# One attention stage of a two-layer kernel rewritten: 32 heads in one stream, key tiles in pairs, the next batch prepared in pieces inside heads

## The chip, the cores and the metric

The kernel runs on one core of one Trainium2 chip. The metric is the device time of one execution, in microseconds. PE is TensorE, PEld its weight load, DVE VectorE, ACT ScalarE, POOL GpSimd, SP SyncE, whose queue issues most DMAs.

## The reference, cut to what matters

Four steps add to x (4 batches of 512 rows, 256 columns): a cross-attention, a mixture of experts, a second cross-attention, a second mixture. The change is in the second cross-attention:

```python
# x: (4, 512, 256), ctx: (4, 1601, 256); 8 heads of 32; Wq, Wk, Wv: (256, 256)
query = _layernorm(x, axis=-1)
q = _split_heads(query @ Wq.T, 8)
k = _split_heads(ctx @ Wk.T, 8)
v = _split_heads(ctx @ Wv.T, 8)
attn = jax.nn.softmax(jnp.einsum('bhnd,bhmd->bhnm', q, k) * 32 ** (-0.5), axis=-1)
x = x + jnp.einsum('bhnm,bhmd->bhnd', attn, v).transpose(0, 2, 1, 3).reshape(B, Nq, C)
```

## The kernel before, in words

`build` calls `attention0`, `experts`, `attention1` and `experts` one after the other; each has its own blocks of engine programs with semaphores written by hand. The stage in question is `attention1`. Numbers are held as sums of two float16 parts, high and low, so that a float32 product becomes three float16 matmuls (`triple`).

Per batch it needs: the context turned (`cth`, `ctl`; 13 tiles of up to 128 rows, the last has 65), keys (`khs`, `kls`), values (`vst`), and, for each head, stacked operands: `kst` holds high, low and high part of the keys on 96 partitions, `qst` high, high and low part of the queries, so that one matmul over 96 rows gives the whole score. Row 97 of `qst` holds the negative row maximum and row 97 of `kst` ones, so the score matmul subtracts the maximum as well. The stacking is done by DMAs from SP, `kst` 24 per batch (L1735), `qst` 24 once for all four batches (L1727).

Order of the work before: an opening normalises all 16 tiles of x (L2040 to L2048), turns weights and x (L1872, L1877), makes all queries (L1859 to L1861) and prepares batch 0. In the function `event(b, i)` the steps of a batch are numbered: 8 turn the context, 8 make keys, 13 make values. Turn and key steps of the next batch run inside the last head of a batch (`NEXT`). The value steps and the stacking of keys run between batches, since there is one `vst` and one `kst`. Then `pre` computes the maxima of the batch's first head (12 matmuls of 512 columns L1962, four of 65 L1955, into two PSUM banks `psA`; DVE reduces them, L2108, L2103, L2093; PE turns the result, L1946; DVE writes it to `qst`, L2097), and the heads run in a loop.

A head (`main`) goes over 13 key tiles. For each, PE makes a score (L1995) into one of four banks `psS`; ACT takes the exponential twice, into float32 `pf` (L1831) and float16 `ph` (L1833); POOL (10 tiles, L1774) or DVE (tiles 2, 6 and 10, L2130) subtracts them to the low part `pl`. Five tiles later PE multiplies the values with `ph` and `pl` into `psO` (L1971, L1973). Beside it runs `pre` for the next head. At tile 5 ACT copies the previous head's `psO` to `of` (L1820), PE folds it (L1983) and DVE divides and adds to X (L2113, L2117). The heads 1 to 6 of a batch are a hardware loop over registers; the batches too.

Of the kernel before, what the change touches and what calls it, by code (L numbers as in the profile page):

```python
# [1592 lines left out]
def attention1(nc, X, identf, io):  # L1593

# [11 lines left out]
    NCK = len(KCH)  # L1606
    NQ = KC * NT // 4 + G * B
    NGC = KC * -(-JT // 4)
    NV0 = NGC + G * NCK
    NW = NV0 + JT  # L1610
    NA = 1 + ST * (NCK - 1)
# [3 lines left out]
    LAG = 5  # L1615
    PR = ring(JT, 7)
    SR = ring(JT, 4)
    R, NS = max(PR) + 1, max(SR) + 1
    VT = [2, 6, 10]
    GT = [j for j in range(JT) if j not in VT]  # L1620

    with ExitStack() as ctx:
        def sb(name, shape, dt=F32):
            return ctx.enter_context(nc.sbuf_tensor("c_" + name, shape, dt))

        def sem(name):
# [16 lines left out]
        cth, ctl = sb("cth", [P, KC, M], F16), sb("ctl", [P, KC, M], F16)  # L1643
        mx, mc = sb("mx", [P, ST, NCK]), sb("mc", [P, ST])
        pf = sb("pf", [P, R, S])
        ph, pl = sb("ph", [P, R, S], F16), sb("pl", [P, R, S], F16)
        of = sb("of", [VC, S])
        fold = sb("fold", [VC, DH + 1])
        rl = sb("rl", [P, ST])

        psA = [ctx.enter_context(nc.psum_tensor(f"c_psA{i}", [P, 512], F32)) for i in range(2)]
        psS = [ctx.enter_context(nc.psum_tensor(f"c_psS{i}", [P, 512], F32)) for i in range(NS)]
        psO = ctx.enter_context(nc.psum_tensor("c_psO", [P, 512], F32))
        psM = ctx.enter_context(nc.psum_tensor("c_psM", [P, 512], F32))
        ring4 = psA + psS[0:2]
# [3 lines left out]
        s_cx = sem("cx")  # L1659
        s_st = sem("st")  # L1660
        s_mv = sem("mv")
        s_pool = sem("pool")
        s_rstd = sem("rstd")
        s_nt = sem("nt")
        s_uP = sem("uP")
        s_uH = sem("uH")
        s_uL = sem("uL")
        s_q = sem("q")
        s_wP = sem("wP")
        s_wH = sem("wH")  # L1670
# [38 lines left out]
        NONE = [[] for _ in range(JT)]
# [503 lines left out]
```

## Time and profile before

| | us |
|---|---|
| median of 3 runs | 2967.51 (2966.61 to 2968.86) |
| the profiled execution | 2967.55 |
| its span, first to last instruction | 2965.7 |
| mean granted TensorE clock | 0.932 |

| engine | busy us | share |
|---|---|---|
| PE | 2521.8 | 85% |
| PEld | 1505.1 | 51% |
| DVE | 1938.1 | 65% |
| ACT | 1728.1 | 58% |
| POOL | 1535.5 | 52% |

The profile is of one execution. Busy shares are means over four stages; names of tiles begin with `a_` in the first attention, `f_` in the experts and `c_` in the second attention. A releaser ("<-") is what ended an idle time. Matmuls overlap: the busy time of one is longer than its distance to the next.

### The profile page before, as it was taken

The numbers are of one execution on the slowest core, as the hardware profiler recorded it, in microseconds if no ns is written. First come the engines' busy times: TensorE is split into PE (matmuls) and PEld (weight loads), VectorE is DVE, ScalarE is ACT, GpSimd is POOL, SyncE is SP. The second block draws the span as 40 slices with busy tenths as digits, with TensorE's granted clock in tenths as the row PEclk, the third lists the DMA queues.
The fourth block names the chain that finished last, engine by engine and source line by source line (L and its number), as shares of the span: only waits on it lengthen the run. The fifth ranks groups of instructions, "written<-read, shape, count | busy, mean of one in ns | idle before, by whom it ended". The sixth has DMA issues, their size and how long they took to land. (4 is left out here: it accounts for less than half of the span.)

```text
span 2965.7 us, 51867 instructions
## 1 busy us (share of the span) xinstructions
PE 2521.8 (85%) x15253; PEld 1505.1 (51%) x15380; DVE 1938.1 (65%) x3676; ACT 1728.1 (58%) x3155; POOL 1535.5 (52%) x1359
## 2 busy tenths in 40 slices
PE   4999999999999999999945991688888888379992
PEld 2455555555555555555424881344344444258882
DVE  5778677776777776677754644675767677656443
ACT  3556656566555665555523750387786868357661
POOL 2576766676676765665744005075665747320004
PEclk9999999999999999999966995799898999579996
DMA  4000000000000000000025413401002010543113
GB/s 130 1 1 1 23 1 1 1 1 23 1 1 1 1 1 1 1 1 1 1 89 180 146 39 97 99 1 30 26 3 52 0 34 0 203 160 117 45 46 93
DMA packets 83500, 122.54 MB, mean 41 GB/s; under 512 B 11139, under 2 KB 67285, under 8 KB 83349
## 3 DMA queue, kind: packets, MB, share of 16 engines
q1 hardware_dynamic: 72020, 86.23, 9.7%
q0 software_dynamic: 9472, 30.16, 3.0%
q10 hardware_dynamic: 1856, 4.19, 0.4%
q8 instruction: 89, 1.46, 0.2%
q14 instruction: 63, 0.51, 0.1%
HBM read 73.23 MB, written 34.34 MB: 36 GB/s over the span
## 5 line engine op out<-in xcount | busy, mean ns | idle before, releaser
L396 POOL TENSOR_TENSOR a_acc<-a_acc,a_pf 128x512 f32<-128x512 f32 (+1 forms) x480 | 644.8, 1343 | 388.0 <-ACT a_pf L524 367.8
L1774 POOL TENSOR_TENSOR c_pl<-c_pf,c_ph 128x512 f16<-128x512 f32 x320 | 386.8, 1227 | 284.7 <-ACT c_ph L1833 282.3
L524 ACT ACTIVATE a_pf<-a_psS 128x1024 f32<-128x1024 f32 (+1 forms) x288 | 281.2, 976 | 303.6 <-PE a_psS L663 300.1
L813 DVE TENSOR_TENSOR a_pl<-a_pf,a_ph 128x512 f16<-128x512 f32 x448 | 404.6, 912 | 27.5 <-ACT a_ph L530 27.5
L789 DVE TENSOR_REDUCE a_mx<-a_psA 128x1 f32<-128x512 f32 x512 | 344.5, 684 | 49.0 <-PE a_psA L600 42.7
L1270 POOL DMA_INDIRECT f_xn<-f_yrows,f_gidx x64 | 60.7, 949 | 506.5 <-DMA f_yrows<-f_xn 487.6
L1831 ACT ACTIVATE c_pf<-c_psS 128x512 f32<-128x512 f32 (+1 forms) x416 | 255.9, 615 | 114.0 <-PE c_psS L1995 110.6
L2108 DVE TENSOR_REDUCE c_mx<-c_psA 128x1 f32<-128x512 f32 x384 | 251.3, 684 | 53.0 <-PE c_psA L1962 51.2
L530 ACT ACTIVATE a_ph<-a_psS 128x1024 f16<-128x1024 f32 (+1 forms) x288 | 281.0, 976 | 0.0
L1833 ACT ACTIVATE c_ph<-c_psS 128x512 f16<-128x512 f32 (+1 forms) x416 | 257.4, 619 | 0.0
L784 DVE TENSOR_TENSOR a_vl<-a_psA,a_vh 128x256 f16<-128x256 f32 (+1 forms) x272 | 115.0, 423 | 167.4 <-ACT a_vh L469 164.4
L1130 DVE TENSOR_TENSOR f_xn<-f_xn 128x256 f16<-128x256 f32 x320 | 132.3, 422 | 130.9 <-ACT f_xn L1106 126.4
L685 PE MATMUL a_psO<-a_pl,a_vh 128*128 128x512 f16 (+1 forms) x544 | 206.7, 380 | 6.9 <-POOL a_pl L401 6.9
L679 PE MATMUL a_psO<-a_ph,a_vh 128*128 128x512 f16 (+1 forms) x544 | 206.9, 380 | 1.0 <-DVE a_ol L818 1.0
L542 PE MATMUL a_psS<-a_qh,a_kh 128*128 128x512 f16 (+1 forms) x544 | 206.6, 380 | 0.9 <-ACT a_mrow L485 0.8
L680 PE MATMUL a_psO<-a_ph,a_vl 128*128 128x512 f16 (+1 forms) x544 | 206.7, 380 | 0.0
L543 PE MATMUL a_psS<-a_ql,a_kh 128*128 128x512 f16 (+1 forms) x544 | 206.7, 380 | 0.0
L544 PE MATMUL a_psS<-a_qh,a_kl 128*128 128x512 f16 (+1 forms) x544 | 206.5, 380 | 0.0
L600 PE MATMUL a_psA<-a_kh,a_qh 128*128 128x512 f16 x512 | 194.3, 380 | 4.7 <-DVE a_kl L778 1.2
L778 DVE SCALAR_TENSOR_TENSOR a_kl<-a_psA,a_bkv,a_kh 128x512 f16<-128x512 f32 (+1 forms) x160 | 105.3, 658 | 133.7 <-ACT a_kh L463 133.6
L1035 PE MATMUL f_psH<-f_xh,f_w 128*128 128x256 f16 x648 | 178.4, 275 | 15.3 <-ACT f_xn L1106 11.7
L1971 PE MATMUL c_psO<-c_ph,c_vst 128*65 128x512 f16 (+1 forms) x416 | 160.8, 386 | 22.7 <-ACT c_of L1820 22.7
(340 smaller groups left out, 6395.2 us busy)
## 6 DMA issues: line engine op xcount, KB each, us to landing
f_stage<-in_L_ffn_w SPq DMA_DIRECT2D x16, 1024.0 KB
f_stage<-in_L_ffn_W SPq DMA_DIRECT2D x16, 1024.0 KB
f_xn<-f_xrows SPq DMA_DIRECT2D x41, 256.0 KB, 2.8
f_yrows<-f_xn SPq DMA_DIRECT2D x40, 256.0 KB, 2.2
c_kst<-c_khs SPq DMA_DIRECT2D x64, 100.1 KB, 2.2
f_xrows<-f_zero POOLq DMA_DIRECT2D x1, 6400.0 KB, 26.4
a_cx<-in_ctx SPq DMA_DIRECT2D x4, 1536.0 KB
c_cx<-in_ctx SPq DMA_DIRECT2D x4, 1536.0 KB
```

Of the source, the lines that this page charges most:

```text
L396: g.tensor_tensor(acc[0:k, p, :], acc[0:k, p, :], pf[0:k, q % RF, i, :], ALU.add).then_inc(s_acc, 1)
L524: act.activation(pf[0:r, q % RF, 0:k, :], psS[q % 2][0:r, 0:k, :], ACT.Exp, scale=SCALE).then_inc(s_pF, 1)
L530: act.activation(ph[0:r, q % RP, 0:k, :], psS[q % 2][0:r, 0:k, :], ACT.Exp, scale=SCALE).then_inc(s_pH, 1)
L543: pe.matmul(out, hi, xl_, start=False, stop=False)
L679: pe.matmul(psO[:, :], vh[0:r, g % 2, j, vs], ph[0:r, q % RP, i, :], start=(j == 0), stop=False)
L680: pe.matmul(psO[:, :], vl[0:r, g % 2, j, vs], ph[0:r, q % RP, i, :], start=False, stop=False)
L789: v.tensor_reduce(mx[:, n % 2, it, c:c + 1], ps[:, 0:KCH[c][1]], AX.X, ALU.max).then_inc(s_fr, 1)
L813: v.tensor_tensor(pl[0:r, q % RP, i, :], pf[0:r, q % RF, i, :], ph[0:r, q % RP, i, :], ALU.subtract).then_inc(s_pL, 1)
L1774: g.tensor_tensor(pl[0:r, PR[j], :], pf[0:r, PR[j], :], ph[0:r, PR[j], :], ALU.subtract).then_inc(s_pG, 1)
L1831: act.activation(pf[0:r, PR[j], :], psS[SR[j]][0:r, :], ACT.Exp, scale=SCALE).then_inc(s_pF, 1)
L1833: act.activation(ph[0:r, PR[j], :], psS[SR[j]][0:r, :], ACT.Exp, scale=SCALE).then_inc(s_pH, 1)
L2108: v.tensor_reduce(mx[:, it, c:c + 1], psA[what % 2][:, 0:cn], AX.X, ALU.max).then_inc(s_aF, 1)
```

## The change

`attention1` is written anew; the other stages are the same to the letter.

- The 32 heads form one stream with no loop: every instruction is written out. The unit is a pair of key tiles (6 pairs and the last tile alone, `UNITS`). `psS` becomes two buffers of two banks, and each exponential covers a pair. `psA` has three banks, used in turn by all steps (`ALL`, `IDX`); `psM` is gone.
- `kst`, `qst` and `vst` have two buffers. `qst` is made per batch, so 48 stacking DMAs per batch go out, six for each head with a semaphore for each head (`s_stack`).
- The next batch is prepared in 25 steps at 22 places of heads 0 to 5 (`PREP_AT`): T turns a chunk of the context, K makes keys, V the values of a pair of tiles, N turns the normalised x, Q makes queries. The context comes in chunks of 512 rows through two buffers, one DMA each.
- The maxima of the next head (M, then L for the last 65 columns, X for the turning) stand at fixed places (`M_AT`). Values lag four units (eight tiles) instead of five tiles; `ph` and `pl` have seven pair buffers, `pf` four.
- The first `item` in the diff is PE's; `out_copy` is DVE's. Subtractions: DVE has two per head (`ON_DVE`), POOL eleven. The copy of `psO` goes from ACT to DVE (`out_copy`). DVE writes the divided output to `yt`, and POOL adds it to X (`add_to_x`).

```diff
-    LAG = 5
-    PR = ring(JT, 7)
-    SR = ring(JT, 4)
-    VT = [2, 6, 10]
+    UNITS = [(j, j + 1) for j in range(0, JT - 1, 2)] + [(JT - 1,)]
+    NB = 3
+    LAG, LATE, RF, RP = 4, 1, 4, 7
+    ON_DVE = {(4, 1), (5, 1)}
+    TOP = U - 1
+    def keys_and_values(b):
+        out = []
+        for c in range(NK):
+            out += [("T", b, c, k) for k in range(KC) if k < parts(c)]
+            out += [("K", b, c, g) for g in range(G) if g < parts(c)]
+            out += [("V", b, u) for u in range(2 * c, min(2 * c + 2, U))]
+        return out
+    def queries(b):
+        return [("N", b, 0), ("N", b, 1), ("Q", b, 0), ("Q", b, 1)]
+    M_AT = [(0, 0), (0, 2), (0, 3), (1, 0), (1, 2), (2, 0), (2, 2), (2, 3), (3, 0), (3, 2), (4, 0), (4, 2)]
+    PREP_AT = [(h, u, p) for h in range(6) for u, p in ((1, 1), (4, 1), (5, 1), (6, 1))]
+    PREP_AT = [(h, u, p) for h, u, p in PREP_AT if (h, u) >= (0, LAG + 1)]
...
+            at[TOP - 1][0].append(("L", n + 1))
+            at[TOP - 1][3].append(("X", n + 1))
+        if n >= 1:
+            at[LAG][2].append(("F", n - 1))
...
-        kst = sb("kst", [P, H, M], F16)
+        kst = sb("kst", [P, 2, H, M], F16)
-        vst = sb("vst", [P, JT, H, VC], F16)
+        vst = sb("vst", [P, 2, JT, H, VC], F16)
-        cx = sb("cx", [P, JT, D])
+        cx = sb("cx", [P, 2, 4, D])
-        psS = [ctx.enter_context(nc.psum_tensor(f"c_psS{i}", [P, 512], F32)) for i in range(NS)]
-        psM = ctx.enter_context(nc.psum_tensor("c_psM", [P, 512], F32))
+        psA = [pb(f"psA{i}", [P, 512]) for i in range(NB)]
+        psS = [pb(f"psS{i}", [P, 2, S]) for i in range(2)]
...
+            for b in range(B):
+                for c in range(NK):
+                    load_context(b, c)
+                stack(b)
...
+            def add_to_x(n):
+                b, h = divmod(n, H)
+                g.wait_ge(s_fr, after_dve(("F", n)))
+                xs = X[:, b * ST:(b + 1) * ST, h * DH:(h + 1) * DH]
+                g.tensor_tensor(xs, xs, yt[:, n % 2, :, :], ALU.add).then_inc(s_x, 1)
...
+            def item(what):
+                i = IDX[what]
+                ps = psA[i % NB]
+                if i >= NB:
+                    pe.wait_ge(s_fr, i - NB + 1)
...
+                for u in range(U):
+                    q = uid(n, u)
+                    places = AT[n][u]
+                    values = tiles_of(q - LAG) if q >= LAG else ()
+                    for i in range(2):
+                        if i < len(UNITS[u]):
+                            score(n, u, i)
+                        for what in places[i]:
+                            item(what)
+                    for i in range(2):
+                        if i < len(values):
+                            value(q - LAG, i)
+                        for what in places[2 + i]:
+                            item(what)
...
+            def out_copy(n):
+                v.wait_ge(s_pv, uid(n, U - 1) + 1)
+                if n >= 1:
+                    v.wait_ge(s_it, IDX[("F", n - 1)] + 1)
+                v.tensor_copy(of[:, :], psO[0:VC, :]).then_inc(s_oF, 1)
```

How the instructions stand now at three places. First PE between two batches, before: the maxima of the batch's first head (L1955, L1962), their turning (L1946), and then the first scores (L1995), each with what it waits for in brackets.

```order
L1955 MATMUL c_psA<-c_kst,c_qst 128x65 [waits c_q,c_aF,c_k0,c_wL]
L1955 MATMUL c_psA<-c_kst,c_qst 128x65 x3
L1962 MATMUL c_psA<-c_kst,c_qst 128x512 [waits c_aF] x12
L1946 MATMUL c_psM<-identf,c_mc 1x128 [waits c_tF,c_mc]
L1946 MATMUL c_psM<-identf,c_mc 1x128 x3
L1995 MATMUL c_psS<-c_qst,c_kst 128x512 [waits c_mr,c_pH,c_k1]
L1955 MATMUL c_psA<-c_kst,c_qst 128x65 [waits c_aF]
L1955 MATMUL c_psA<-c_kst,c_qst 128x65 x3
L1962 MATMUL c_psA<-c_kst,c_qst 128x512 [waits c_aF]
L1995 MATMUL c_psS<-c_qst,c_kst 128x512 [waits c_pH]
L1962 MATMUL c_psA<-c_kst,c_qst 128x512 [waits c_aF]
```

Now the same place, the end of head 7 and the start of head 8: the turning (L1999), the last score of head 7 (L2017), values (L2034, L2039), the first score of head 8, and a maximum of head 9 (L1987).

```order
L1999 MATMUL c_psA<-identf,c_mc 1x128 [waits c_mc,c_fr]
L1999 MATMUL c_psA<-identf,c_mc 1x128 x3
L2017 MATMUL c_psS<-c_qst,c_kst 65x512 [waits c_pH]
L2034 MATMUL c_psO<-c_ph,c_vst 65x512 [waits c_pH]
L2039 MATMUL c_psO<-c_pl,c_vst 65x512 [waits c_pG,c_pL]
L2034 MATMUL c_psO<-c_ph,c_vst 65x512
L2039 MATMUL c_psO<-c_pl,c_vst 65x512
L2017 MATMUL c_psS<-c_qst,c_kst 128x512 [waits c_fr,c_pH]
L1987 MATMUL c_psA<-c_kst,c_qst 128x512 [waits c_stack1,c_fr]
L2017 MATMUL c_psS<-c_qst,c_kst 128x512
```

The block of twelve maxima in a row is gone; between the scores of two batches stand four value matmuls, and the wait is for the stacking of head 9, not of the whole batch.

Second, PE where the previous head's `psO` must have been copied (`c_oF`). Before, at tile 5 of a head: a value of the previous head (L1973), a score, a maximum, the new head's first value (L1971).

```order
L1973 MATMUL c_psO<-c_pl,c_vst 65x512 [waits c_pG]
L1992 REGISTER_ALU
L1995 ISA [waits c_pH]
L1995 MATMUL c_psS<-c_qst,c_kst 128x512
L1951 REGISTER_ALU
L1962 MATMUL c_psA<-c_kst,c_qst 128x512 [waits c_aF]
L1971 ISA [waits c_oF,c_pH]
L1971 MATMUL c_psO<-c_ph,c_vst 65x512
L1698 ISA
L1973 MATMUL c_psO<-c_pl,c_vst 65x512 [waits c_pG]
```

Now, in unit 4 of head 7 (one of a batch's two heads without preparation): a score, a maximum, a score, the first value (L2034), a maximum, the fold (L2004), the unit's second tile, and the next unit.

```order
L2017 MATMUL c_psS<-c_qst,c_kst 128x512 [waits c_pH]
L1987 MATMUL c_psA<-c_kst,c_qst 128x512 [waits c_fr]
L2017 MATMUL c_psS<-c_qst,c_kst 128x512
L2034 MATMUL c_psO<-c_ph,c_vst 65x512 [waits c_oF,c_pH]
L2039 MATMUL c_psO<-c_pl,c_vst 65x512 [waits c_pG,c_pL]
L1987 MATMUL c_psA<-c_kst,c_qst 128x512 [waits c_fr]
L2004 MATMUL c_psA<-c_fold,c_of 128x33 [waits c_oF,c_fr]
L2004 MATMUL c_psA<-c_fold,c_of 128x33 x3
L2034 MATMUL c_psO<-c_ph,c_vst 65x512
L2039 MATMUL c_psO<-c_pl,c_vst 65x512
L2017 MATMUL c_psS<-c_qst,c_kst 128x512 [waits c_pH]
L1993 MATMUL c_psA<-c_kst,c_qst 128x65 [waits c_fr]
```

In heads 1 to 5 a preparation step stands ahead of that first value, behind the second score. The copy itself has moved from ACT to DVE.

Third, SP. Before, the keys of a batch are the last of 24 DMAs; the load of the next batch's context follows.

```order
L1735 DMA c_kst<-c_khs 32x1601
L1741 REGISTER_ALU
L1717 ISA [waits c_wP]
L1717 DMA c_cx<-in_ctx 128x12x256
L1719 ISA
L1719 DMA c_cx<-in_ctx 65x256
L1738 REGISTER_ALU
```

Now the last of the 48 stacking DMAs of batch 0 (keys L1790 and queries L1791 in turn) and the first chunks of batch 1's context (L1776).

```order
L1790 DMA c_kst<-c_khs 32x1601 [waits c_fr]
L1791 DMA c_qst<-c_qhs 32x512
L1790 DMA c_kst<-c_kls 32x1601
L1791 DMA c_qst<-c_qhs 32x512
L1790 DMA c_kst<-c_khs 32x1601
L1791 DMA c_qst<-c_qls 32x512
L1776 DMA c_cx<-in_ctx 128x4x256 [waits c_it] x3
L1778 DMA c_cx<-in_ctx 65x256 [waits c_it]
```

So the first load for batch 1 has 48 issues ahead of it in SP's queue instead of 24 for keys alone (after 24 for queries).

## Rows read from the trace of the kernel before

**Rows 1.** Windows: busy us (x) of PE, PEld, DVE, ACT, POOL; clock, DMA share, GB/s.

```profile
1836.40:1882.70 46.30, 19.35 (x92) 12.37 (x92) 35.08 (x67) 11.02 (x19) 15.49 (x9) 0.67 0.17 53
1882.70:1926.00 43.30, 32.31 (x173) 17.73 (x173) 23.28 (x45) 14.16 (x30) 0.00 (x0) 0.79 0.69 168
1962.50:1978.30 15.80, 13.60 (x68) 6.85 (x67) 12.08 (x24) 13.61 (x28) 12.18 (x11) 1.00 0.00 0
2044.50:2064.00 19.50, 17.05 (x91) 8.24 (x90) 7.89 (x18) 13.15 (x28) 7.82 (x7) 1.00 0.07 16
2064.00:2087.00 23.00, 17.26 (x107) 10.47 (x107) 15.28 (x33) 6.95 (x15) 0.00 (x0) 0.82 0.63 166
2087.00:2107.30 20.30, 20.19 (x76) 7.77 (x76) 16.38 (x26) 18.03 (x37) 14.82 (x13) 0.78 0.00 0
```

**Rows 2.** Timeline at the first seam: start, length, instruction, [idle before <-what ended it].

```profile
2075.19 0.60 SPq L1735 DMA_DIRECT2D c_kst<-c_kls  x1
2075.83 0.60 SPq L1735 DMA_DIRECT2D c_kst<-c_khs  x1
2087.64 0.60 ACT L1831 ACTIVATE c_pf<-c_psS 128x512 f32<-128x512 f32 x1 [13.01 <-PE c_psS L1995]
```

**Rows 3.** Waits in three plain heads (1962.5 to 2010): total us, times, longest.

```profile
PE c_psM L1946 <- DVE c_mc L2093: 3.5, 3, 1.2
PE c_psO L1971 <- ACT c_of L1820: 2.5, 3, 0.8
```

**Rows 4.** Timeline, PE in a plain head.

```profile
1983.70 0.38 PE L1971 MATMUL c_psO<-c_ph,c_vst 128*65 128x512 f16 x1
1983.92 0.38 PE L1973 MATMUL c_psO<-c_pl,c_vst 128*65 128x512 f16 x1
...
1986.35 0.60 PE L1946 MATMUL c_psM<-identf,c_mc 128*1 128x128 f32 x4 [1.18 <-DVE c_mc L2093]
```

**Rows 5.** Timeline, ACT: 512 columns here, 1024 columns in the first attention.

```profile
368.71 1.02 ACT L524 ACTIVATE a_pf<-a_psS 128x1024 f32<-128x1024 f32 x1 [0.17 <-PE a_psS L663]
369.63 0.38 ACT L469 ACTIVATE a_vh<-a_psA 128x256 f16<-128x256 f32 x1
...
1985.38 0.67 ACT L1833 ACTIVATE c_ph<-c_psS 128x512 f16<-128x512 f32 x1
1985.86 0.68 ACT L1831 ACTIVATE c_pf<-c_psS 128x512 f32<-128x512 f32 x1
```

**Rows 6.** By source line: ns min/median/max of one, first and last start, forms.

```profile
L1774 POOL TENSOR_TENSOR c_pl<-c_pf,c_ph x320: 1147/1155/1609, 1928.0 to 2530.3; 128x512 f16<-128x512 f32 x160
L2130 DVE TENSOR_TENSOR c_pl<-c_pf,c_ph x96: 679/735/1643, 1931.1 to 2528.2; 128x512 f16<-128x512 f32 x96
L362 POOL TENSOR_TENSOR X<-X,a_yt x128: 716/728/1277, 155.4 to 1508.6; 128x256 f32<-128x256 f32 x128
```

**Rows 7.** Timeline: the opening of the second attention, and its last instruction.

```profile
1847.23 16.11 DVE L2048 TENSOR_SCALAR c_qst<-X,c_mv,c_rstd 128x256 f32<-128x256 f32 x16 [3.58 <-POOL c_rstd L1752]
...
1914.77 0.57 PE L1955 MATMUL c_psA<-c_kst,c_qst 96*128 96x65 f16 x4 [1.33 <-DVE c_vst L2082]
1925.97 0.59 PE L1995 MATMUL c_psS<-c_qst,c_kst 97*128 x1 [1.09 <-DVE c_qst L2097]
...
2533.94 0.73 DVE L2117 SCALAR_TENSOR_TENSOR X<-c_psM,c_rl,X 128x32 f32<-128x32 f32 x4
```

**Rows 8.** The page, DMA issues: KB each, median us from issue to landing.

```profile
c_kst<-c_khs SPq DMA_DIRECT2D x64, 100.1 KB, 2.2
a_vl<-in_L_xattn_Wq ACTq DMA_DIRECT2D x1, 1024.0 KB, 5.5
```

**Rows 9.** Timeline, PE at the lower clock level, after the seam.

```profile
2088.41 0.63 PE L1962 MATMUL c_psA<-c_kst,c_qst 96*128 96x512 f16 x1
2088.83 0.63 PE L1995 MATMUL c_psS<-c_qst,c_kst 97*128 x1
```

**Rows 10.** The page: TensorE's granted clock in tenths, 40 slices of 74.1 us.

```profile
PEclk9999999999999999999966995799898999579996
```

More of the change, by code:

```diff
@@ new lines, in last_turn, with last_keys, after_act, after_dve @@
+    def last_turn(b, c):
+        return IDX[("T", b, c, parts(c) - 1)]
+    def last_keys(b, g):
+        return max(IDX[("K", b, NK - 2, g)], IDX[("K", b, NK - 1, 0)])
+    def after_act(what):
+        return AH[IDX[what]]
+    def after_dve(what):
+        return IDX[what] + 1
+    PER_DVE = len(ON_DVE)
+    PER_POOL = JT - PER_DVE
+    def low_dve(q):
+        n, u = divmod(q, U)
+        return n * PER_DVE + sum(1 for w in range(u + 1) for i in range(len(UNITS[w])) if (w, i) in ON_DVE)
+    def low_pool(q):
+        n, u = divmod(q, U)
+        return n * PER_POOL + sum(1 for w in range(u + 1) for i in range(len(UNITS[w])) if (w, i) not in ON_DVE)
@@ L1647, in attention1 @@
         of = sb("of", [VC, S])
         fold = sb("fold", [VC, DH + 1])
[L1649 to L1655 removed]
+        rl = sb("rl", [P, 2, ST])
@@ new lines, in item, with score @@
+                ins.then_inc(s_it, 1)
+            def score(n, u, i):
+                q, j = uid(n, u), UNITS[u][i]
+                b, h = divmod(n, H)
+                r = rows1(j)
+                if i == 0:
+                    if q >= 2:
+                        pe.wait_ge(s_pH, q - 1)
+                    if u == 0:
+                        pe.wait_ge(s_fr, after_dve(("X", n)))
+                ins = pe.matmul(psS[q % 2][0:r, i, :], kst[0:KR, b % 2, h, j * P:j * P + r], qst[0:KR, b % 2, h, :],
+                                start=True, stop=True)
+                if i == len(UNITS[u]) - 1:
+                    ins.then_inc(s_sP, 1)
@@ new lines, in value @@
+            def value(q, i):
+                n, u = divmod(q, U)
+                b, h = divmod(n, H)
+                j = UNITS[u][i]
+                r = rows1(j)
+                if i == 0:
+                    pe.wait_ge(s_pH, q + 1)
+                    if u == 0 and n >= 1:
+                        pe.wait_ge(s_oF, n)
+                if h == 0 and i == 0:
+                    pe.wait_ge(s_fr, after_dve(("V", b, u)))
+                w = vst[0:r, b % 2, j, h, :]
+                pe.matmul(psO[0:VC, :], w, ph[0:r, q % RP, i, :], start=(j == 0), stop=False)
+                if i == 0:
+                    if low_dve(q):
+                        pe.wait_ge(s_pL, low_dve(q))
+                    pe.wait_ge(s_pG, low_pool(q))
+                ins = pe.matmul(psO[0:VC, :], w, pl[0:r, q % RP, i, :], start=False, stop=(j == JT - 1))
+                if i == len(UNITS[u]) - 1:
+                    ins.then_inc(s_pv, 1)
@@ new lines, in _ @@
+            norm(0, "xs")
+            norm(0, "xa")
+            norm(0, "nx")
+            for what in OPEN + FIRST:
+                item(what)
+            for n in range(NH):
+                b, h = divmod(n, H)
+                for u in range(U):
+                    q = uid(n, u)
+                    places = AT[n][u]
+                    if n >= 1 and u == LAG:
+                        out_copy(n - 1)
+                    for i in range(2):
+                        low(q - LATE, i)
+                        for what in places[i]:
+                            item(what)
+                    for what in places[2] + places[3]:
+                        item(what)
+                    if b + 1 < B and (h, u) in NORM_AT:
+                        norm(b + 1, NORM_AT[h, u])
@@ L2156, in build @@
+            for q in range(NH * U - LATE, NH * U):
+                for i in range(len(tiles_of(q))):
+                    low(q, i)
+            out_copy(NH - 1)
+            for what in CLOSE:
+                item(what)
 def build(nc, io, out, phases):
```

777 lines of the change are left out of this document (346 added, 431 removed).

## Prediction

> **What bounds the kernel now.** The change touches one stage of four, so I first cut the run by stage with the windows [rows 1]. The second attention lasts from 1836.4 us to the end of its last addition at 2534.7 [rows 7]: 698.3 of 2965.7. Its first score stands at 1926.0 [rows 7], so the opening takes 89.6 and the 32 heads 608.7. A plain head takes 15.8: PE is busy 13.6, ACT 13.6, POOL 12.2, DVE 12.1, at full granted clock. No engine is full. The reader should see the seam instead: 23.0 us (2064 to 2087) in which POOL does nothing and ACT 7.0, followed by a head at clock 0.78 that takes 20.3 instead of 15.8. ACT waits 13.0 for the first score of the new batch [rows 2]. Head 7, which prepares part of the next batch, takes 19.5 [rows 1]. Seven plain heads and such a seam make the batch 161 us, 34 more than eight plain heads.
>
> Then the waits of three plain heads [rows 3]: PE stands 1.2 us per head for the column maxima (`mc`) before the transposes, and 0.8 per head for the copy of psO. A matmul's busy time overlaps the next one's; what it costs PE is the start-to-start time, 0.217 us for 512 columns [rows 4].
>
> **Part by part.** *PE's work per head* is unchanged: 13 scores, 26 value and 12 maxima matmuls, 51 x 0.217 = 11.1; four transposes of mc 0.43 (four take 0.60, the last 0.27 of it is drain [rows 4]); four 65-column maxima 0.5 and four folds 0.9, both estimates from the same timeline. Sum 12.9, against 15.8 taken.
>
> *ACT.* 26 exponentials become 12 of 1024 columns and two of 512. Start to start, 1024 columns take 0.92, 512 take 0.48 [rows 5]: 12.0 us per head, where 26 x 0.48 = 12.5 plus a psO copy of 0.48 stood before. The copy goes to DVE, for which no row has a price; between ACT's 0.59 and a DVE subtraction of 0.74 [rows 6] I take 0.65, on DVE's 12.1 us [rows 1], which loses one subtraction and the four additions to X. DVE stays near 11.5.
>
> *POOL* gets 11 subtractions instead of 10, and the addition to X. Alone a subtraction takes 1.15, beside a DVE subtraction up to 1.61, and DVE's own then goes to 1.64 [rows 6]. I take 11 x 1.12 (start to start) + 2 x 0.4 for the two met by DVE's + 0.45 for an addition half as wide as the 0.73 one [rows 6]: 13.5 per head. Now a rule against this move: the Trainium skill's GPSIMD Engine Reference, section Key points, says that for elementwise work DVE is structurally about twice as fast. The trace agrees at 1.155 against 0.735. By the rule, with that one subtraction left on DVE, POOL's head would be 12.4. Either way POOL lies under the PE figure below, so the sum stands; the rule feeds the rival in which POOL leads.
>
> *Waits in a plain head.* Maxima come in pairs of units with three banks instead of two, and the last of them (65 columns) is followed by a score and four value matmuls before the transposes, 1.1 us, as long as DVE's two short reductions: the wait of 1.2 goes. The copy of psO stays: PE finishes the previous head's last value, issues one maximum, two scores and another (0.87) and then needs the copy, while DVE first reduces the maximum and then copies, some 1.9 from the same point. PE waits 1.0 to 1.1. With 0.2 for the rest a plain head takes 12.9 + 1.3 = 14.2. Bounds: POOL's 13.5, and today's 15.8.
>
> *Preparation in heads.* Per batch PE gets 36 matmuls of 512 (7.8) and twelve of 65 (0.4) for K, 78 of 256 columns at half the pitch (8.5) for V, 34 transposes at 0.108 (3.7), 12 of 512 (2.6) for Q: 23.0 us, in heads 0 to 5. Nothing hides these on PE, because PE is already the longest engine; they hide ACT's and DVE's share (25 steps of about 0.48 and 0.65). They also hide the psO copy in heads 1 to 5, where such a step stands ahead of the value. Heads 0 to 5 together: 6 x 12.9 + 23.0 + 1.1 + 6 x 0.25 = 103. In ACT's order a preparation copy stands between the two exponentials of a unit and waits for its own matmuls; I follow a unit: PE 3.0, ACT 0.92 + 0.7 idle + 0.48 + 0.92 = 3.0. It just fits, so the bounds are 16.9 and 19 per head.
>
> *The stream.* A batch is 103 + 2 x 14.2 = 131.4, three times 394; the last batch 7 x 14.2 + 12.0 (no maxima, ACT's time) = 111.4. The three seams disappear, because the next head's maxima find their stacked rows ready: SP starts the 48 stacking DMAs at the end of head 5, one each 0.64 us [rows 2], landing 2.2 later [rows 8]; head 0's six are in after 6 us, heads 6 and 7 last 28.
>
> One new wait, once. In batch 0 SP issues all 48 stacking DMAs (30.7 us) before the load of batch 1's first chunk, 512 KB, which lands some 4 later (1 MB took 5.5 [rows 8]). PE wants that chunk in unit 5 of head 0. With everything stacked from 1882.5 on, the chunk is there at 1917.5 and PE asks at 1909.5: 8 us. Behind the wait the clock falls, as it did after each seam; I add 4. In later batches the same 30.7 us end about 8 us ahead of the request. Draining the last units, fold and addition add 3. Together 394 + 111.4 + 8 + 4 + 3 = 520.4.
>
> *The opening.* Norms, transposes and Q of batch 0 alone: the scaling of 16 tiles, 16.1 us [rows 7], becomes 4, done by 1845 instead of 1863. Then 25 steps on PE, in three banks: 25 us of matmuls (the 23.0 above and the turning of the weights) plus five chains of 1.8 (a K or Q needs the DVE half of the transposes before it) plus 3 at the low clock, to 1882.5. Six DMAs and their landing 6.0; the first head's maxima took 11.2 (1914.8 to 1926.0 [rows 7]). First score at 1899.7, the opening 63.3 instead of 89.6. The two memsets of kst on POOL hide behind this; they end near 1862.
>
> Sum: 63.3 + 520.4 = 583.7 against 698.3, so 114.6 less. The profiled execution took 2967.55 (span 2965.7), the median of the runs is 2967.51, no different. 2967.5 - 114.6 = 2852.9; the first maxima at the low clock may cost a little more, so I say **2854**.
>
> **The rivals.**
> *Engines in step (chance 0.21).* In-order ACT and a POOL near 13.5 of 14.2 lose to each other what the seams give: plain heads stay at 15.8, preparing heads take 19. Stream 3 x (114 + 31.6) + 7 x 15.8 + 12 + 15 = 574.4, so 2967.5 - 60.6 = 2907. For it: before, PE also had 12.9 of work and took 15.8. Against it: there it waited for maxima, which now have room [rows 3].
>
> *Everything hides (0.12).* Plain heads at POOL's 13.5, preparing ones 16.9, no late chunk, an opening of 56: 3 x 128.4 + 106.5 + 3 = 494.7, so 2820.
>
> *The clock oscillates (0.04), slower than before.* At the lower level a matmul of 512 columns starts every 0.43 us [rows 9]; 51 of them take 21.9, a plain head about 24, 10 more. From twelve of the 32 heads on, the gain of 114 is gone; with all of them at 1.2 GHz, and 23 more in each of three batches, the run takes 2854 + 320 + 69 = 3243. For it: small waits in each head. Against it: the first attention, written in this same pattern, keeps the full level from slice 2 to slice 20 [rows 10]. The rule is in the Trainium skill, TensorE: Matmul & The Clock Gate, section A second HAM failure mode: psum-queue depth-cycling: a kernel that cycles through PSUM banks idles so often that its clock oscillates. The trace so far disagrees: plain heads cycle banks at 1.00 [rows 1].
>
> *The seam moves rather than goes (0.05).* If SP's 48 DMAs arrive late in every batch and not once, PE loses 8 + 4 twice more: 2878.
>
> **How the numbers follow.** The forecast has the remaining 0.58. Faster than by 0.2% (about 6 us, what a measurement of this kernel tells from none) are all but the clock rival and the far end of the first: 0.95; the same 0.01; slower 0.04. The range takes the forecast with the bounds of its heads (14 plain ones at +-0.6, 18 preparing ones at +-0.8: +-23), the late seams and most of the rival at 2907: 2826 to 2905; outside are the clock, the best case and the worst half of the first rival.
>
> **What would show it.** A span near 2851; first score near 1900; psO copies 14.2 apart in heads 6, 7 and the last batch and 17 apart in heads 1 to 5; no POOL gap of 25 us at a batch's start; one wait of about 8 us of PE for `c_cx` in head 0; the wait for `mc` gone and that for the psO copy near 1 in plain heads alone; clock 1.00 after the first 60 us of the stream. Plain heads at 15 or more with POOL full, or a clock under 0.95 in the stream, would show me wrong.

## The result and the profile after

| | before | after |
|---|---|---|
| median | 2967.27 | 2898.69 (2896.74 to 2899.26) |
| ratio, 95% interval | | 0.9767 (0.975 to 0.9784) |
| span of the profiled execution | 2965.7 | 2894.9 |
| second attention in it, first instruction to last addition | 1836.4 to 2534.7: 698.3 | 1833.9 to 2466.3: 632.4 |
| opening, to its first score | 89.6 | 77.8 |

The change is worth 68.6 us; I forecast 113. In the two profiled executions the second attention gives 65.9 of it. What lies outside it is 2267.4 before and 2262.5 after: its code is the same, and in the profiles of the experiments below it lies between 2263 and 2268.

The stream is there. POOL has no gap between batches, the 13.0 us in which ACT waited for a new batch [rows 2] are gone, and so are the two dips to 8 in the stream's later part of the clock's row [rows 10]. The page after:

```profile
PEclk9999999999999999999985998589999999579996
```

The windows after: the opening, one plain head (of batch 0, from the psO copy in head 6 to that in head 7), and the next one, up to the copy in head 0 of batch 1 (columns as in [rows 1]):

```profile
1833.90:1911.70 77.80, 37.93 (x205) 21.76 (x205) 50.13 (x55) 16.48 (x29) 24.61 (x10) 0.70 0.19 52
2040.00:2053.40 13.40, 12.63 (x67) 6.69 (x67) 11.91 (x22) 12.27 (x15) 13.40 (x13) 1.00 0.46 107
2053.40:2071.00 17.60, 14.43 (x67) 7.13 (x67) 14.57 (x21) 12.43 (x15) 13.98 (x14) 0.90 0.48 126
```

A plain head takes 13.4, less than my 14.2. But the next one, with the same 67 matmuls, takes 17.6. The starts of the copies of psO in the timeline, one per head, give the beat of the whole stream. In the second batch they are 17.1, 22.0, 21.5, 15.2, 16.0, 13.4, 17.7, 17.6 apart: 140.5 for eight heads, where I had 131.4. The list of waits says who holds PE. PE over the stream (1911.7 to 2466.3), total us, times, longest:

```profile
PE c_psS L2017 <- DVE c_qst L2139: 13.9, 7, 2.4
PE c_psO L2034 <- DVE c_of L2165: 13.6, 20, 0.8
PE c_psA L1946 <- DVE c_mx L2132: 11.0, 3, 3.7
PE c_psA L1946 <- DMA c_cx<-in_ctx: 9.0, 1, 9.0
```

The second and the fourth row I had expected, the first and the third not; nor the length of the opening. All three surprises have DVE as releaser, and at each POOL is busy. In the opening (timeline after):

```profile
1837.34 22.50 DVE L2086 TENSOR_SCALAR c_xn<-X,c_mv,c_rstd 128x256 f32<-128x256 f32 x4 [1.59 <-POOL c_rstd L1804]
1837.37 21.62 POOL L1812 MEMSET c_kst<- 1x12808 f16 x2
1860.50 1.97 PE L1946 MATMUL c_psA<-identf,c_cx 128*128 128x128 f32 x8 [18.80 <-DVE c_wtl L2102]
```

Four scalings of a tile last as long as POOL's two memsets, and PE waits 18.8 us. At the end of head 7 of batch 0:

```profile
2057.09 0.17 DVE L2092 TENSOR_REDUCE c_mc<-c_mx 128x4 f32<-128x16 f32 x1
2057.18 3.53 DVE L2158 TENSOR_TENSOR c_pl<-c_pf,c_ph 128x512 f16<-128x512 f32 x1
2057.49 0.46 POOL L1835 TENSOR_TENSOR X<-X,c_yt 128x128 f32<-128x128 f32 x1
2057.90 3.82 POOL L1823 TENSOR_TENSOR c_pl<-c_pf,c_ph 128x512 f16<-128x512 f32 x3
2060.75 0.68 DVE L2139 TENSOR_SCALAR c_qst<-c_psA 1x512 f16<-1x512 f32 x1
2061.58 0.38 PE L2017 MATMUL c_psS<-c_qst,c_kst 97*128 97x512 f16 x1 [2.38 <-DVE c_qst L2139]
```

A subtraction that takes DVE 0.68 alone lasts 3.53, while POOL starts one instruction behind the other. The write of the maxima into `c_qst` stands behind it, and the first score of the next batch behind that. Five heads have such a wait of 2.4, a sixth one of 1.2; around three of the five the clock falls to 0.5 for 3.4 us.

The subtraction does not wait for a gap of POOL's, though I took it so at first. POOL works without one from 2035.02 to 2061.72:

```profile
2035.02 8.95 POOL L1823 TENSOR_TENSOR c_pl<-c_pf,c_ph 128x512 f16<-128x512 f32 x8 [1.23 <-ACT c_ph L1916]
2043.91 0.91 POOL L1835 TENSOR_TENSOR X<-X,c_yt 128x128 f32<-128x128 f32 x1
2044.79 12.74 POOL L1823 TENSOR_TENSOR c_pl<-c_pf,c_ph 128x512 f16<-128x512 f32 x11
```

In the same stretch two earlier subtractions of DVE, at the turn from head 6 to head 7, got in behind the one POOL instruction then under way:

```profile
2043.74 0.77 DVE L2158 TENSOR_TENSOR c_pl<-c_pf,c_ph 128x512 f16<-128x512 f32 x1
2045.43 1.06 DVE L2158 TENSOR_TENSOR c_pl<-c_pf,c_ph 128x512 f16<-128x512 f32 x1
```

The one at 2057.18 let four POOL instructions end before it (one under way, the addition, two subtractions) and got done beside the third subtraction, which then took 1.60 instead of 1.15.

In head 3, where the next batch's tiles are scaled:

```profile
1979.29 6.93 POOL L1823 TENSOR_TENSOR c_pl<-c_pf,c_ph 128x512 f16<-128x512 f32 x6 [0.18 <-ACT c_ph L1916]
1981.33 3.88 DVE L2086 TENSOR_SCALAR c_xn<-X,c_mv,c_rstd 128x256 f32<-128x256 f32 x4
1985.13 1.28 DVE L2132 TENSOR_REDUCE c_mx<-c_psA 128x1 f32<-128x512 f32 x2
1985.87 1.11 PE L1946 MATMUL c_psA<-identf,c_cx 128*128 128x128 f32 x4 [3.67 <-DVE c_mx L2132]
```

Here each of the last three scalings takes 1.24, one POOL subtraction long, and not 0.40.

Theory, as I had it before the experiments: DVE's operations whose operands all lie in SBUF starve while POOL works without a gap, and what stands behind them on DVE is what PE wants. Rivals: the order of the work, or a resource (a bank, PE itself, POOL's throughput) sets these times.

### The profile page after: what moved, and what is told of

The parts are those of the page before. It is cut to its first block and busy times, and to the rows that moved or that the text cites. A ratio compares the mean times of both kernels' runs of the same rounds, so it can differ in the third digit from the quotient of the medians.

```text
span 2894.9 us, 47028 instructions
## 1 busy us (share of the span) xinstructions
PE 2482.1 (86%) x15253; PEld 1505.0 (52%) x15380; DVE 1966.7 (68%) x3548; ACT 1678.3 (58%) x2705; POOL 1585.6 (55%) x1430
## 3 DMA queue, kind: packets, MB, share of 16 engines
q8 instruction: 106, 1.74, 0.3%
## 5 line engine op out<-in xcount | busy, mean ns | idle before, releaser
L1823 POOL TENSOR_TENSOR c_pl<-c_pf,c_ph 128x512 f16<-128x512 f32 (+1 forms) x352 | 409.0, 1189 | 152.0 <-ACT c_ph L1916 151.2
L813 DVE TENSOR_TENSOR a_pl<-a_pf,a_ph 128x512 f16<-128x512 f32 x448 | 422.6, 952 | 28.8 <-ACT a_ph L530 28.8
L1910 ACT ACTIVATE c_pf<-c_psS 128x1024 f32<-128x1024 f32 (+1 forms) x224 | 216.7, 968 | 85.8 <-PE c_psS L2017 83.8
L1916 ACT ACTIVATE c_ph<-c_psS 128x1024 f16<-128x1024 f32 (+1 forms) x224 | 216.4, 966 | 0.0
L1036 PE MATMUL f_psH<-f_xl,f_w 128*128 128x256 f16 x648 | 178.6, 276 | 0.0
## 6 DMA issues: line engine op xcount, KB each, us to landing
f_xrows<-f_zero POOLq DMA_DIRECT2D x1, 6400.0 KB, 26.7
```

The source lines that it names most:

```text
L813: v.tensor_tensor(pl[0:r, q % RP, i, :], pf[0:r, q % RF, i, :], ph[0:r, q % RP, i, :], ALU.subtract).then_inc(s_pL, 1)
L1036: pe.matmul(ps, a, xl[:, p, k, :], start=False, stop=False)
L1823: g.tensor_tensor(pl[0:r, q % RP, i, :], pf[0:r, q % RF, i, :], ph[0:r, q % RP, i, :], ALU.subtract).then_inc(s_pG, 1)
L1910: act.activation(pf[0:r, q % RF, 0:k, :], psS[q % 2][0:r, 0:k, :], ACT.Exp, scale=SCALE).then_inc(s_pF, 1)
L1916: act.activation(ph[0:r, q % RP, 0:k, :], psS[q % 2][0:r, 0:k, :], ACT.Exp, scale=SCALE).then_inc(s_pH, 1)
```

## The experiments

Each kernel is the changed kernel with one edit, or a combination of such; each was timed beside the kernel before (2966.1 to 2967.5). The ratio is to that kernel, with its 95% interval.

### e1: load the next chunks ahead of stacking

```diff
             for b in range(B):
-                for c in range(NK):
+                for c in range(2 if b else 0, NK):
                     load_context(b, c)
+                if b + 1 < B:
+                    load_context(b + 1, 0)
+                    load_context(b + 1, 1)
                 stack(b)
```

> Only SP's order changes: the first two chunks of the next batch's context are loaded ahead of the 48 stacking DMAs. The changed kernel took 2898.7. Theory (the late chunk costs PE 9.4 us once, at 1930.7, and then a clock of 0.5 for 10.2 us, worth 5): 14 less, 2885, with no PE wait for c_cx and no clock fall at 1926. Rival (a wait behind it takes its place, the stacked rows coming 4 us later, or the chunk is late for another reason): 2895 to 2900.

Measured 2888.64, ratio 0.9736 (0.9719 to 0.9752): 10.1 less, not 14. The wait for `c_cx` and the clock's fall at 1926 are gone. In their place stands a shorter wait a little later, before the keys made of that chunk:

```profile
PE c_psA L1926 <- DVE c_ctl L2111: 1.5, 1, 1.5
```

The clock was priced too high: in the changed kernel the lower level held from 1926.4 to 1936.6, but PE only worked again from 1930.7 on, 5.9 us at half speed, so 3 and not 5. Counted from start to start, less the 0.22 of a matmul, the two waits are 9.2 and 1.7: 9.2 + 3 - 1.7 is 10.5.

### e2: memsets behind the scaling

```diff
                 if i == 4:
                     rstds(0)
                     g.wait_ge(s_rstd, 1)
+                    g.wait_ge(s_st, NORMED["nx"])
```

> Only POOL's two memsets of c_kst (21.6 us) wait until DVE has scaled the four tiles c_xn. In the changed kernel the four scalings took 22.5 us, over just the stretch of the memsets (1837.3 to 1859.8), and PE idled 18.8. Theory (POOL's memset starves a DVE operation whose operands all lie in SBUF): the scalings take 4 x 0.4 = 1.6 us, the first score comes 15 to 18 us earlier, the memsets end near 1861 and hide; 2898.7 - 17 = 2882. Rival A (the scalings are slow for another reason, such as X not yet being there): they stay at 22 and the time stays at 2899 or rises. Rival B (DVE's operations from PSUM starve just as much under the memset): the loss moves to c_wtl and c_ctl and the time stays within 5 us of 2899.

Measured 2879.91, ratio 0.9706 (0.969 to 0.9722): 18.8 less. The timeline:

```profile
1839.35 1.38 DVE L2087 TENSOR_SCALAR c_xn<-X,c_mv,c_rstd 128x256 f32<-128x256 f32 x4 [1.59 <-POOL c_rstd L1804]
1840.85 21.59 POOL L1813 MEMSET c_kst<- 1x12808 f16 x2 [1.54 <-DVE c_xn L2087]
1842.86 0.69 DVE L2103 SCALAR_TENSOR_TENSOR c_wtl<-c_psA,c_wth 128x512 f16<-128x512 f32 x1 [2.14 <-ACT c_wth L1863]
```

22.5 us became 1.38 by nothing but the order of two engines. Rival B falls with the third row: under the same memset, a DVE operation that reads PSUM takes its plain 0.69. The Trainium skill, SBUF — State Buffer, section SBUF: two separate sides, says that DVE and GpSimd share a port pair by an exclusive lock, held for the whole instruction, and that whichever starts first keeps it; on DVE's side it names two-port modes and operations with two SBUF inputs, the latter only against a GpSimd operation that reads SBUF. The trace after agrees on the length: the longest scaling lasted 10.94, a memset 10.8. A memset reads nothing, so by this rule of the Trainium skill only a two-port mode could make the scaling wait; which of DVE's modes it used no run shows.

### e3: DVE's subtractions behind the write

```diff
-    ON_DVE = {(4, 1), (5, 1)}
+    ON_DVE = {(5, 0), (5, 1)}
```

> The two subtractions that DVE does are those of the unit (5,0), (5,1) instead of (4,1), (5,1), so that both stand behind the write of the maxima into c_qst and none ahead of it; POOL still has 11. Theory (the 2.8 us waits of PE for c_qst at the end of five heads are a DVE subtraction of up to 3.5 us, starved by POOL, that the write stands behind; each also costs 3.4 us at clock 0.5): 5 x (2.5 + 1.7) = 21 less, 2878; no PE wait over 1 us for c_qst. Rival (the write is late because the maxima before it are): the waits stay and so do 2899 +- 4. A second rival: the subtractions are still starved and now hold up the first maxima of the next head: 2890 to 2905 with waits for c_mx at unit 0.

Measured 2900.67, ratio 0.9773 (0.9757 to 0.9789): no gain; the second rival came true. No score waits for `c_qst`, plain heads are all alike, but at 14.8. Waits of PE in one (2365.9 to 2380.7):

```profile
PE c_psA L1987 <- DVE c_mx L2132: 1.2, 1, 1.2
PE c_psO L2034 <- DVE c_of L2165: 0.8, 1, 0.8
```

The two subtractions now take up to 1.7 each at the head's end, and the next head's maxima stand behind them. Moving the starved operation moved the wait.

### e4: the scaling in four places

The diff, cut:

```diff
-    NORM_AT = {(2, 0): "xs", (2, 2): "xa", (3, 2): "nx"}
+    NORM_AT = {(2, 0): "xs", (2, 2): "xa"}
+    NX_AT = {(3, 1): 0, (3, 6): 1, (4, 1): 2, (4, 6): 3}
```

> The scaling of the next batch's four tiles (c_xn) on DVE is spread over four places in heads 3 and 4 instead of standing in one. Theory (the PE waits of 4.06 us at 1985.9, 2127.6 and 2268.1 are the 3.9 us of these four scalings, with the maxima behind them; each is followed by 6.8 to 10.2 us at clock 0.5): 3 x 3.8 + 13.6 (half of 27.2 us) = 25 less, 2874; clock falls at 1984, 2128, 2268 gone. Rival (the waits are small, the clock falls have another cause): only 11 less, 2887. Other rival (each single scaling costs its 1 us on PE anyway): 2895.

Measured 2887.81, ratio 0.9731 (0.9715 to 0.9747): 10.9 less, the number of the first rival, but not for its reason: the waits of 3.7 are gone and so are the clock falls behind them. Heads 2 and 3 of the second batch go from 22.0 and 21.5 to 19.1 and 19.9, 4.4 less, and those of the other two give 5.2 and 5.8. In exchange starved subtractions cost 4 us more from the end of the third batch on. And 25 was too much from the start: I had added up clock time in which PE stood still anyway, as in e1, and taken for granted that each scaling would then be free.

### f1: loads, memsets and scaling together

The diff is those of e1, e2 and e4.

> Three edits together: the next batch's first two chunks loaded ahead of stacking (10.1 less alone), the memsets of c_kst behind the scaling of c_xn (18.8 less), c_xn spread over four places (10.9 less). Theory (they lie in different places and simply add): 2898.7 - 39.8 = 2859, first score near 1894 - 2 = 1892 if the loads have cost the opening nothing. Rival (the clock, which falls behind each long wait, gives back more once the waits are gone): 2850. Rival (a wait that one removes is taken up by the next): 2868.

Measured 2859.17, ratio 0.9635 (0.9619 to 0.9651): the gains add.

### f2: a third subtraction on DVE

```diff
-    ON_DVE = {(4, 1), (5, 1)}
+    ON_DVE = {(3, 1), (4, 1), (5, 1)}
```

(on f1)

> As f1_three, and DVE takes a third subtraction per head, (3,1); POOL 10 instead of 11. Theory (a plain head of 13.44 is POOL's 11 x 1.11 + 0.45 + what it loses to DVE's subtractions, so POOL leads; and DVE's subtraction starves only as long as POOL has no gap): POOL's head 12.9, PE's 12.9 + waits leads, plain heads near 13.2 with fewer ends of 17.6: f1_three less 8. Rival (DVE's subtractions cost more where they stand than POOL gains, since each can hold up the maxima behind it by 1 to 3.5 us): f1_three plus 10 to 25.

Measured 2838.23, ratio 0.9566 (0.955 to 0.9581): 20.9 less than f1, far more than the 8 expected. All waits over 2 us for `c_qst` are gone, and with them the clock falls: after 1896 one is left, of 6.8 us. The page's clock:

```profile
PEclk9999999999999999999995699689999999589996
```

The window of one plain head:

```profile
2328.10:2341.50 13.40, 12.61 (x67) 6.70 (x67) 12.34 (x22) 12.26 (x15) 13.10 (x12) 1.00 0.00 0
```

It takes 13.4, as before, so the gain is not a shorter plain head. DVE's 96 subtractions have a median of 0.69 and none over 1.7, where the changed kernel's 64 had 0.98 and 3.57. What goes with it is POOL's gap in each plain head: its longest stretch without one is 8.3 there, where the changed kernel's six longest waits lie in stretches of 26.7 to 27.2. But the length of the stretch does not give the wait: in f4 one of 12.8 holds a subtraction of 2.93, in e3 stretches up to 13.7 hold none over 1.74. The edit also moves DVE's other work against POOL's, and no run separates the two. By source line, f2 and then the changed kernel:

```profile
L2163 DVE TENSOR_TENSOR c_pl<-c_pf,c_ph x96: 677/694/1683, 1901.0 to 2399.4; 128x512 f16<-128x512 f32 x96
```

```profile
L2158 DVE TENSOR_TENSOR c_pl<-c_pf,c_ph x64: 681/980/3570, 1922.8 to 2458.3; 128x512 f16<-128x512 f32 x64
```

### f3: all subtractions on POOL

```diff
-    ON_DVE = {(4, 1), (5, 1)}
+    ON_DVE = set()
```

(on f1)

> As f1_three, and POOL does all 13 subtractions of a head, DVE none. Theory (POOL leads the plain heads, DVE's subtraction starves): all waits of PE over 2 us for c_qst vanish, plain heads take 13 x 1.112 + 0.45 = 14.9 each, evenly; heads 0 to 5 of a batch, at 15.5 or more, hardly change. 14 plain heads of 14.9 against a mixture of 13.4 and 17.7 with a mean near 14.8 in the last batch: f1_three +-6. Rival A (POOL does not lead): heads of 13.4 with no wait for c_qst, f1_three less 20. Rival B (POOL lags in preparing heads too, since PE's values wait for it): every head 0.5 longer, f1_three plus 15.

Measured 2852.59, ratio 0.9616 (0.96 to 0.9632), 6.6 less than f1, just outside the +-6. No wait for `c_qst` is left, and the plain heads of the last batch take 14.9, evenly, with POOL full:

```profile
2341.80:2356.60 14.80, 13.15 (x67) 6.34 (x67) 10.21 (x19) 12.39 (x15) 14.80 (x16) 1.00 0.00 0
```

This is what POOL as the leader looks like, and it costs: from the first psO copy of the last batch to its last it takes 103.3, 3.1 more than f1. That f3 beats f1 all the same comes from the three batches with preparation, 131.9, 132.0 and 129.2 instead of 136.5, 136.5 and 132.3: the waits for `c_qst` at the ends of their head 7 are gone, and their plain heads take 13.4 and 13.6, not 14.9.

### f4: one key tile as unit

The diff, cut (places and rings renumbered to match):

```diff
-    UNITS = [(j, j + 1) for j in range(0, JT - 1, 2)] + [(JT - 1,)]
+    UNITS = [(j,) for j in range(JT)]
-    LAG, LATE, RF, RP = 4, 1, 4, 7
-    ON_DVE = {(4, 1), (5, 1)}
+    LAG, LATE, RF, RP = 8, 2, 8, 14
+    ON_DVE = {(9, 0), (11, 0)}
-        psS = [pb(f"psS{i}", [P, 2, S]) for i in range(2)]
+        psS = [pb(f"psS{i}", [P, 1, S]) for i in range(4)]
```

> One part of the change undone in the changed kernel: the unit is one key tile (four score banks of 512 columns, exponentials of 512), all else as before at the same places; DVE's two subtractions are those of tiles 9 and 11. ACT then has 26 x 0.48 = 12.5 us of a plain head instead of 12.0, and 14 more instructions. Theory (POOL leads with 13.4, ACT lies under it in plain heads; preparing heads are led by PE): within 6 us of 2898.7. Rival (the pairs are what let the engines run on: with single tiles each copy of a preparation step meets ACT nearly full, and plain heads go to 14.5, preparing ones 1.5 longer): 14 x 1 + 18 x 1.5 = 41 more, 2940.

Measured 2904.81, ratio 0.9791 (0.9774 to 0.9807): 6.1 more, at the edge of the theory and far from the rival's 2940. Plain heads take 13.7 instead of 13.4. The three batches with preparation take 4.5 to 5.3 more each, where the four scalings now take 5.47 and PE waits up to 5.9 for the copy of psO behind them. The last batch takes 6.7 less, because three waits of 2.2 for `c_qst` stand where five of 2.4 stood, none of them in it. So the run prices the pairs together with that, and not alone; what it shows of the pairs is the 0.3 per plain head.

### h1: copy psO ahead of the maximum

```diff
-                    if n >= 1 and u == LAG:
-                        out_copy(n - 1)
 ...
+                    if n >= 1 and u == LAG - 1:
+                        out_copy(n - 1)
                     for what in places[2] + places[3]:
                         item(what)
```

(on f2)

> As f2_three_dve3 (2838.2), and DVE copies psO before the last maximum of the unit ahead, instead of behind it. Theory (a plain head of 13.44 is PE's work, 12.4, plus a wait of 0.97 for this copy, which stands behind a maximum of 0.68): the wait falls to about 0.3, plain heads to 12.8; 14 plain heads and some of the 18 preparing ones: 14 x 0.68 = 10 less, up to 14; 2824 to 2829. Rival (POOL, 10 x 1.11 + 0.45 + 3 x 0.45 = 12.9, or what DVE's subtractions do to it, sets 13.4): 2838 +-3, with waits for c_pl in place of those for c_of. Rival (the maximum, now later, holds its bank and PE waits for that): 2838 +-3 with waits for c_mx.

Measured 2834.93, ratio 0.9558 (0.9542 to 0.9574), 3.3 less than f2, where 10 was forecast. The intervals of the two ratios overlap, and 2.9 of the difference is f2's one clock fall. The copy's wait is gone from the plain heads, as the theory said, but they only fall to 13.36. In one of them the longest wait of PE now is

```profile
PE c_psA L2004 <- DVE c_mc L2097: 0.5, 1, 0.5
```

so the wait moved, as in the second rival but to another place: the last maxima, which DVE now ends later.

### h2: two psA banks

```diff
-    NB = 3
+    NB = 2
```

(on f2)

> As f2_three_dve3 (2838.2), with two psA banks instead of three, the number that the kernel before had. My prediction put the wait of 1.2 us per head for the column maxima down to the two banks, and let it go with the third. Theory: each maxima item waits for the item two before it, whose matmul, reduction of 0.68 and signals take about 1.1; PE spaces them by 0.65 to 1.1: 0.5 to 3 us more per plain head, 1 to 4 in preparing heads, where PE, ACT and DVE take a bank in turn: 31 x 2 = 60 more, 2900. Rival (the order of the maxima within the units did it, not the bank): under 10 more, 2848.

Measured 2898.75, ratio 0.9776 (0.976 to 0.9792): 60.5 more, as the theory had it. But not by its route: a plain head goes only from 13.44 to 14.20, and PE does not wait for the maxima before the transposes:

```profile
PE c_psO L2039 <- DVE c_of L2170: 0.8, 1, 0.8
PE c_psS L2022 <- DVE c_qst L2144: 0.4, 1, 0.4
```

The third bank is worth 10 us in the opening, 11 to 16 in each of the three batches with preparation (plain heads included), and under 1 in a plain head.

### h3: the addition to X on DVE

The diff, cut:

```diff
-                                add_to_x(what[1])
 ...
+                if what[0] == "F":
+                    v.wait_ge(s_fr, after_dve(what))
+                    v.tensor_tensor(xs, xs, yt[:, what[1] % 2, :, :], ALU.add).then_inc(s_x, 1)
```

(on f2)

> As f2_three_dve3 (2838.2), with the addition to X on DVE instead of POOL. POOL's head goes to 10 x 1.11 + 3 x 0.45 = 12.5, DVE's gets one more operation whose operands all lie in SBUF (0.3 alone), right ahead of the last maxima. Theory (POOL does not lead any more, and such an operation on DVE waits for a gap of POOL's): no gain; where it is starved, the reduction behind it and the write into c_qst come later: 0 to 1 us per head more, 2838 to 2860. Rival (POOL leads still): 2838 - 14 x 0.4 = 2832 or less.

Measured 2855.06, ratio 0.9628 (0.9612 to 0.9644): 16.8 more. Plain heads take 14.6; the 1.2 more is a wait for the maxima that stand behind the addition on DVE:

```profile
PE c_psA L2003 <- DVE c_mc L2096: 1.0, 1, 1.0
```

### h4: a place for each preparation step

```diff
-    PREP_AT = [(h, u, p) for h in range(6) for u, p in ((1, 1), (4, 1), (5, 1), (6, 1))]
+    PREP_AT = [(h, u, p) for h in range(6)
+               for u, p in ((1, 1), (3, 1), (4, 1), (5, 1), (6, 1)) if u != 3 or h in (1, 2, 3)]
```

(on h1)

> As h1_copy, and the 25 preparation steps of a batch get a place of their own each (25 places instead of 22, three places more in heads 1, 2 and 3), so that no place holds two. Theory (the preparing heads take 8 us per batch more than 6 x 13.44 + 23.0 less 6 copy waits; two steps in one place, in banks taken in turn, are a part of it): 1 us per doubled place, 9 in all: h1_copy less 9. Rival (a step at a place of unit 3 meets the psO copy and the maxima on DVE): h1_copy +-3 or a few more.

Measured 2834.24, ratio 0.9554 (0.9538 to 0.957), 0.7 less than h1: no difference. The three heads of a batch that changed take 18.2, 19.0 and 18.8 instead of 17.2, 19.4 and 20.0: the same work, dealt out otherwise. h1 and h4 are the fastest: 64 us below the changed kernel and 131 to 132 below the one before.

## Why the prediction was right in sign and short in size

The forecast (2854, range 2826 to 2905) had the mechanism: the seams go, the batches flow, one late chunk. The sum missed by 44.7, in these steps. "Clean" is f2, where no operation of DVE waits for long.

| step | forecast | after | clean |
|---|---|---|---|
| opening | 63.3 | 77.8 | 57.8 |
| plain head | 14.2 | 13.44, or 17.6 | 13.44 |
| heads 0 to 5 of a batch | 103 | 109.4 (batch 1) | 105.8 |
| late chunk, with its clock | 12 | 12.2 | gone |
| second attention | 583.7 | 632.4 | 572.8 |

- **The opening** failed at "the scaling of 16 tiles, 16.1 us [rows 7], becomes 4" and at "the two memsets of kst on POOL hide behind this". I divided 16.1 by 16. The trace of before gives another picture by source line (ns min/median/max) and by timeline:

```profile
L2048 DVE TENSOR_SCALAR c_qst<-X,c_mv,c_rstd x16: 396/400/10940, 1847.2 to 1862.9; 128x256 f32<-128x256 f32 x16
```

```profile
1847.25 10.77 POOL L1757 MEMSET c_kst<- 1x12808 f16 x1
```

One scaling took 10.94, beside the memset of 10.77, one 0.72 and fourteen 0.40. There was one such memset before, and now there are two: 1.6 us of scaling became 22.5. Forecast 63.3, measured 77.8, +14.5. Without that the opening is 58.4 (e2) and 57.8 (f2): my walk through its 25 steps was some 5 too slow, which hid part of the miss.

- **The plain head** failed in its terms, not in its form. Four 65-column maxima were priced at 0.5; they start at 2056.31 and the next score at 2056.43, 0.12. The folds, 0.9, take 0.81. With 51 x 0.217 and 0.44 for the transposes PE's work is 12.4, not 12.9. The wait for the psO copy is 0.97 from start to start (0.81 of it idle) against 1.0 to 1.1. 12.4 + 1.0 is the 13.4 of f2. Thirteen such heads: 10 less than forecast.

- **POOL** was called "under the PE figure below, so the sum stands". As a throughput this is just right (f3 shows the head that POOL leads, 14.9; with 11 subtractions the head is 13.4), but PE's head came out at 13.4 and not 14.2, and in it POOL is busy 13.40 of 13.40. But beside a nearly full POOL, DVE's operations wait: a subtraction with 11 of them on POOL (the changed kernel) up to 3.57, with 10 (f2) at most 1.68. The row for it stood in [rows 6], 0.735 at the median against 1.643: I priced it as 0.4 on POOL for each meeting, and never asked how long DVE would wait, nor what is queued behind it. This is the step that cost most. The writes that came late cost 5 x 2.5 + 1.4, and 3 x 1.7 for the clock, together 19; the scalings in head 3, against the same heads of f2, 14.

- **Preparation** in clean heads takes 105.8, not 103: 2.8 in each of three batches, 8. The term was further off than that: with the plain head's work as measured, 12.4, the same sum gives 100, and 5.8 per batch is without a cause. h4 shows that doubled places are not it. What is stays open.

- **The late chunk** was right: forecast 8 + 4, measured 9.2 + 3; e1, which undoes it, gains 10.1.

Opening 14.5, late writes 19, scalings 14, preparation 8, less 10 for the plain heads: 46 of the 48.7 by which the second attention missed its 583.7. The last 4 of difference to the 44.7 lies outside of it.

- **The wait for the column maxima** is gone, as forecast, but one of my two reasons falls: with two banks (h2) it is gone as well in plain heads. So the bank did not do that; that the order of the maxima did is what is left of my reasons, and no run tested it. The third bank pays in the opening and in the preparing heads. Of the 2.4 us by which a plain head became shorter than the 15.8 of before, the bank gives 0.8 and the pairs 0.3; the rest was not taken apart.

- **The rivals.** "Engines in step", 2907, is the nearest in time and wrong in cause: plain heads at a steady 15.8 do not occur. That 2898.7 lies in the range is luck: the bounds of the heads end at 2877, the rest was for late seams and for this rival, and neither came. (At the other end, 2826 is 5 below what +-23 gives.) My sign of being wrong, plain heads at 15 or more with POOL full, did show, in three plain heads of 17.6 and one of 16.0, though they are long by one wait each and not by an even POOL. "Everything hides", 2820, is what f2 and h1 come near to, by 13.4 per plain head. The clock does not oscillate: in the stream it falls for 3.4 to 10.2 us at a time, behind the long waits, and has a mean of 0.95. I had expected 1.00 after 60 us, and it came only with f3, h1, h3 and h4, and with f2 but for one fall. A chunk behind SP's stacking is late once and never again.

- **A reading of the kernel before.** Beside the seam of 23.0, a batch of 161 us held not seven plain heads but five at 15.8, one of 20.3 behind the seam, and 18.7 and 19.5 for the two at its end. The total was right, and no term hangs on it.

## What to carry to other kernels

Before work is moved to POOL, list DVE's operations that have all their operands in SBUF, and see what is queued behind each. How long such an operation waits was read here neither from POOL's busy share nor from its stretch without a gap: it was one POOL instruction in most places and four in five of them. So look for the row of the operation itself, beside POOL's. Read min, median and max of a group, not its mean: one instruction of 10.9 us among others of 0.4 is a wait on another engine, and it does not shrink with the work. An engine just under the bound may still be the one to relieve: one subtraction less per head on POOL gave 20.9 us with plain heads of the same length.

## What I had not expected of the hardware

- A DVE subtraction can wait for more than one POOL instruction: 3.53 us (0.68 alone), past an addition and two subtractions that POOL started after it. The Trainium skill, SBUF — State Buffer, section SBUF: two separate sides, has the lock for one instruction, and that whoever starts first gets it. In the trace after, this fits the subtractions of 0.77 and 1.06 and the scalings of 1.24, and not the five of 3.5. What lets POOL pass DVE there stays open.
- A scaling took 10.94 beside a memset of one partition's row.
- DVE operations that read PSUM took 0.69 under the same memset (e2).
- POOL pays as well where DVE gets in: its subtraction takes 1.60 instead of 1.15.
- With a wait of PE of 2.4 us went, in three places of five, a stretch of 3.4 us at clock 0.5 (1.2 GHz); in f1 with all four such waits. In f2, without the long waits, the clock stays at 1.00 (2.4 GHz) for 344.7 us; then it falls once, for 6.8 us, behind a wait of 0.95 for the psO copy that stands at the same place in the two batches before, where nothing followed. What tips it stays open.
